# Transposes by DMA, side matmuls in halves, value batches in pairs: a fused transformer block on one core

## The chip, the core and the metric

The kernel runs on 1 core of one Trainium2 chip. The metric is the device time of one execution in microseconds: 1193.36 before the change, the median of 3 runs (1192.19 to 1194.55). The core has TensorE (PE, its weight loads are PEld), VectorE (DVE), ScalarE (ACT), GpSimd (POOL) and SyncE (SP, here the issuer of nearly all DMAs). Each engine works through its own stream of instructions in order; semaphores order them against each other.

## The reference, cut to what matters

The input x has 4096 rows of 256. Three residual steps follow each other (a macaron block):

```python
x = x + 0.5 * ffn(layernorm(x))
x = x + attention(layernorm(x))     # 16 heads of size 16, causal, 4096 x 4096 scores per head
x = x + 0.5 * ffn(layernorm(x))

# attention: k, q, v = x Wk', x Wq', x Wv'; k and q get a layernorm per head (gain, bias), times 256**-0.25
#            out = softmax(causal(q k')) v, then out Wo' + bo
# ffn:       base = x W' + b;  logits = x router', softmax, the two largest of 6, made to sum to 1
#            inner = x A' (7 experts of rank 16, one of them shared), weighed, times B', added to base
```

## The kernel before

**Chunks and stages.** The rows are cut into 8 chunks of 512 (4 tiles of 128). Around the attention of chunk c the kernel does side work for other chunks, in stages with names: `front` (first feed-forward: moments0, scale0, turn0, inner0, route0, weigh0, turnin0, outer0), `prepare` (moments1, scale1, turn1, qk, square and squares, roots, value, norm, heads), `output` (turnout, projout) and `back` (moments2 to outer1). While chunk c is in attention, the side work is `prepare(c+1)`, a front, `output(c-1)` and `back(c-2)`. The first two fronts and most of `prepare` of chunks 0 and 1 stand before any attention, in the prelude; the string PRELUDE gives its order.

**Attention.** The scores come in 1056 units; most are two heads times one tile of 128 keys times 512 queries. A unit is 2 score matmuls in f16 into two banks of PSUM, one exponential by ScalarE over 128 x 1024 (line 776) into a slot of `ring` (5 slots in f32), and later a share of a values batch: 4 heads, so two units, 8 recorded f32 matmuls (one values batch) that add into bank ACC. There are 544 batches. Scores stand two units ahead of the exponential, in 3 pairs of banks (SLOTS). The units of chunks 0 to 7 number 20, 52, 84, 116, 148, 180, 212 and 244.

**Order.** `schedule` writes one global order. For each unit: exp, mask, side stages of place 3u, scores(u+2), side stages of place 3u+1, values, side stages of place 3u+2. PLACES says for each chunk and each kind of side work at which place, in thirds of a unit, each stage stands. Every engine takes its part of each stage out of this one order, so a matmul of a side stage stands in PE's stream between scores and values.

**Transposing on PE.** `turn` (line 1232) transposes normed rows, f32, 128 x 256 pairs: four 128 x 128 transposes into one bank, twice per chunk and layer norm. `turn_inner` (line 1252) does four for the weighed inner product. The f32 result is then split into an f16 part and an f16 rest (`move_parts`, lines 846 and 848, the first by ScalarE in some chunks, line 765), because the side matmuls are done as three f16 products. `turn_heads` (line 1298) transposes q and k, VectorE gives them gain and bias (line 1013) and casts (1017), POOL makes the rest (537), SP writes the parts to DRAM and reads them back into `keys` and `queries`.

**Queues.** SP issues all these DMAs in the same global order and waits for the semaphore of each in that order. All side stages but those of the prelude and of the end share one PSUM bank (SIDE).

**The prelude.** VectorE does moments and `scale` (line 828); POOL squares qk (line 532) into the one buffer `sq`, and VectorE sums them (985), by turns. ScalarE squares the weights for their sizes (line 752), three at the start and four when stage sizes 1 comes. The first score follows the whole prelude.

## Time and profile before

| | before |
|---|---|
| median of 3 runs | 1193.36 us |
| span of the profiled execution | 1192.3 us |
| PE busy / PEld busy | 1104.1 / 359.6 us |
| ACT busy, of it exponentials | 1014.7, 982.2 us |
| DVE / POOL busy | 467.5 / 241.6 us |
| first exponential starts, last starts | 96.3, 1158.4 us |

The page gives for each engine the busy time and its share of the span, and the span in 40 slices with a digit each. A group's line has line, engine, operation, output<-input, shapes and count, then busy us and mean ns of one, then the idle time just before it and who ended that. The profiled execution has no time of its own beside its span; it is 1.1 us under the median.

### The profile page before, as it was taken

How to read it: one execution, taken by the hardware profiler on the slowest of the kernel's cores; microseconds unless marked ns; L12 is line 12 of the kernel's file. 1: busy time of each engine (PE TensorE's matmuls, PEld its weight loads, DVE VectorE, ACT ScalarE, POOL GpSimd, SP SyncE). 2: the span in 40 equal slices, each digit the busy share in tenths (PEclk: the TensorE clock that was granted, in tenths of full speed). 3: DMA queues.
4: the chain of work that ended last, by engine and by line, in shares of the span. 5: the costliest groups of instructions: out<-in, count | busy, mean ns of one | idle time of the engine just before them, and what ended most of it. 6: DMA issues, size and time to landing. Idle time of an engine off the chain costs nothing.

```text
span 1192.3 us, 22761 instructions
## 1 busy us (share of the span) xinstructions
PE 1104.1 (93%) x8884; PEld 359.6 (30%) x8884; DVE 467.5 (39%) x1181; ACT 1014.7 (85%) x1134; POOL 241.6 (20%) x377
## 2 busy tenths in 40 slices
PE   3758999999999999999999999999999999999994
PEld 3534333332323233232332232232222222222123
DVE  5678665554544353333333323423131222021114
ACT  3216788789888998999999999999999999999980
POOL 2236533222122211212022021012110101010100
PEclk9779999999999999999999999999999999999996
DMA  5022202003000300003000022000001100000000
GB/s 145 3 63 60 59 11 81 1 28 99 1 1 19 93 17 1 1 32 92 4 1 1 1 67 60 1 1 2 1 10 48 53 1 1 10 10 1 1 19 18
DMA packets 39608, 33.37 MB, mean 28 GB/s; under 512 B 8722, under 2 KB 39432, under 8 KB 39496
## 3 DMA queue, kind: packets, MB, share of 16 engines
q1 hardware_dynamic: 37364, 31.74, 9.0%
q8 instruction: 73, 1.20, 0.4%
q10 hardware_dynamic: 2132, 0.12, 0.1%
q14 instruction: 39, 0.32, 0.1%
HBM read 18.73 MB, written 12.85 MB: 26 GB/s over the span
## 4 chain that ended last, share of the span: by engine, by line
PE 72%; ACT 13%; issue 6%; DVE 6%; DMA 1%; POOL 1%; SPq 0%; ACTq 0%; DVEq 0%; POOLq 0%
PE ps L1190 68%; ACT ring L776 13%; PE ps L1232 2%; PE ps L1298 1%; DMA x<-in_x 1%; DVE st L807 1%; PE ps L1252 1%; DVE area L828 1%; DVE oT L1159 0%; POOL rstd L711 0%; POOL sq L532 0%; DVE x L980 0%; DVE ss L985 0%; DVE sq L1013 0%; ACT area L765 0%
## 5 line engine op out<-in xcount | busy, mean ns | idle before, releaser
L776 ACT ACTIVATE ring<-ps 128x1024 f32<-128x1024 f32 x1056 | 982.2, 1115 | 65.5 <-PE ps L1190 63.5
L1190 PE MATMUL ps<-ring,vf 128*17 128x512 f32 (+3 forms) x4608 | 559.4, 562 | 5.0 <-DVE oT L1159 4.4
L1190 PE MATMUL ps<-queries,keys 50*128 50x512 f16 (+3 forms) x2304 | 363.2, 366 | 22.1 <-ACT ring L776 4.9
L1190 PEld LDWEIGHTS ps<-queries,keys 50*128 50x128 f16 x2304 | 92.3, 93 | 475.3 <-ACT ring L776 437.3
L724 POOL TENSOR_SCALAR_AFFINE_SELECT ring<-ring 128x256 f32<-128x256 f32 (+1 forms) x224 | 103.9, 481 | 396.5 <-ACT ring L776 392.6
L1190 PEld LDWEIGHTS ps<-ring,vf 128*17 128x17 f32 x4608 | 79.7, 95 | 174.5 <-issue 144.2
L711 POOL TENSOR_TENSOR rstd<-var,minus_half 128x4 f32<-128x4 f32 x24 | 24.4, 1017 | 235.6 <-DVE var L813 235.4
L980 DVE SCALAR_TENSOR_TENSOR x<-ps,power,x 128x512 f32<-128x512 f32 x32 | 24.0, 750 | 110.7 <-PE ps L1190 110.7
L846 DVE CAST xnT<-ps 128x512 f16<-128x512 f32 x32 | 22.1, 691 | 100.0 <-PE ps L1232 100.0
L1190 PE MATMUL ps<-baseT,xnT 128*128 128x256 f16 x384 | 55.0, 283 | 3.9 <-DVE area L848 3.8
L1232 PE MATMUL ps<-ident,area 128*128 128x128 f32 x192 | 34.2, 311 | 20.0 <-DVE area L828 20.0
L765 ACT ACTIVATE xnT<-ps 128x512 f16<-128x512 f32 x16 | 9.6, 599 | 49.9 <-PE ps L1232 49.9
L1159 DVE STREAM_TRANSPOSE oT<-ps 128x512 f32<-128x512 f32 x32 | 22.9, 715 | 71.0 <-PE ps L1190 70.5
L1190 PE MATMUL ps<-qkT,xnT 128*128 128x512 f16 x192 | 48.7, 394 | 1.7 <-DVE xnT L848 1.5
L532 POOL TENSOR_TENSOR sq<-area 128x512 f32<-128x512 f32 x32 | 33.5, 1047 | 67.2 <-DVE ss L985 41.7
L1190 PEld LDWEIGHTS ps<-baseT,xnT 128*128 128x128 f16 x384 | 36.7, 101 | 19.2 <-issue 11.0
L828 DVE TENSOR_SCALAR area<-x,mv,rstd 128x256 f32<-128x256 f32 x96 | 36.9, 444 | 11.3 <-POOL rstd L711 11.3
L1013 DVE TENSOR_SCALAR sq<-ps,scaled 128x512 f32<-128x512 f32 x16 | 12.9, 806 | 70.1 <-PE ps L1298 70.1
L537 POOL TENSOR_TENSOR split<-sq,split 128x512 f16<-128x512 f32 x16 | 18.8, 1175 | 100.0 <-DVE split L1017 100.0
L807 DVE BATCH_NORM_STATS2 st<-x 128x6 f32<-128x256 f32 x96 | 33.5, 412 | 9.5 <-DMA x<-in_x 4.8
L1232 PEld LDWEIGHTS ps<-ident,area 128*128 128x128 f32 x192 | 23.6, 156 | 43.0 <-issue 36.9
L848 DVE TENSOR_TENSOR xnT<-ps,xnT 128x512 f16<-128x512 f32 x48 | 33.1, 691 | 7.6 <-ACT xnT L765 6.3
(153 smaller groups left out, 670.5 us busy)
## 6 DMA issues: line engine op xcount, KB each, us to landing
parts_d<-split SPq DMA_DIRECT2D x32, 256.0 KB, 2.6
keys<-parts_d SPq DMA_DIRECT2D x96, 64.0 KB, 2.3
queries<-parts_d SPq DMA_DIRECT2D x192, 32.0 KB
x<-in_x SPq DMA_DIRECT2D x8, 512.0 KB, 4.2
out_x<-x SPq DMA_DIRECT2D x16, 256.0 KB, 2.2
queries<-shift_d SPq DMA_DIRECT2D x64, 4.0 KB
ring<-in_base_W SPq DMA_DIRECT2D x1, 256.0 KB, 4.9
ring<-in_Wq SPq DMA_DIRECT2D x1, 256.0 KB, 3.8
```

Of the source, the lines that this page charges most:

```text
L532: e.tensor_tensor(sq[:, :], qn[:, n % TC, :], qn[:, n % TC, :], ALU.mult).then_inc(K.sq_ok, 1)
L711: pool.tensor_tensor(rstd[ln][:, :], var[ln][:, 0, :], minus_half[:, :].broadcast_to([P, TC]), ALU.pow).then_inc(main.rstd_ok[ln], 1)
L724: m = pool.affine_select(out=tiles[:, part, :], in_=tiles[:, part, :], compare_op=ALU.is_ge, fill=0.0, base=0, pattern=[[0, len(range(8)[p ...
L776: act.activation(probs[:, u % RING, :], bank(2 * (u % SLOTS), 2), ACTF.Exp, bias=0.0, scale=1.0).then_inc(exp_ok, 1)
L807: dve.bn_stats(st[ln][:, i, :], x[:, i, :]).then_inc(*own.up())
L828: m = dve.tensor_scalar(xn[ln][:, i, :], x[:, i, :], mv[ln][:, i, 0:1], rstd[ln][:, i:i + 1], ALU.subtract, ALU.mult)
L846: dve.tensor_copy(high, src).then_inc(*K.own.up())
L848: dve.tensor_tensor(low, src, high, ALU.subtract).then_inc(K.read, 1)
L980: dve.scalar_tensor_tensor(out=x, in0=bank(K.bank[key]).rearrange("p (n d) -> p n d", n=2), scalar=power[0][:, 5:6], in1=x, op0=ALU.mult, ...
L1159: dve.transpose(oT[:, :], bank(ACC)).then_inc(acc_read, 1)
L1190: return pe.matmul(o, lhsT, rhs, start=start, stop=stop, skip_group_check=True)
L1232: m = pe.transpose(b[:, ib * D + i * P:ib * D + (i + 1) * P], xn[ln][:, 2 * a + i, ib * P:(ib + 1) * P], ident[:, :])
```

## The change

- **Transposes by DMA.** `by_queue` says which: turn0 and turnin0 from chunk 3 on, turn1 from chunk 2 on, turn2 and turnin1 up to chunk 6. For these, DVE (ScalarE where it did before) makes the f16 part and rest from SBUF before the transpose, into the unused half of `area`, and SP issues one `dma_start_transpose` (`turn_rows`, `turn_hrows`) of 128 x 1024 f16. PE issues no transpose and waits for the landing before the next side matmul (`wait_turned`). POOL clears the unused columns first. `xnT` is laid out anew by tile.
- **Halves.** Side matmul stages (qk, value, projout, inner, outer) of later chunks are two stages each with places of their own.
- **Pairs.** `held_back` holds a values batch back until the next one, where HELD has a 1 (88 of them); `ring` gets a sixth slot, for which `split` falls from four buffers to two (a head block waits until the write of the block before the last has landed).
- **ScalarE in the prelude.** scale0 of chunks 0 to 2 and scale1 of chunk 0, the squares of chunk 0 from PSUM, the heads of chunk 0 (two passes each), and all seven weights' squares at the start. Squares use two buffers (`qT[n % 2]`).
- `addbo` stands behind the heads; PRELUDE and all of PLACES are new (the prelude's string has 100 entries and had 102; the half stages add positions).

```diff
-RING = 5
+SCALAR_SCALES, SCALAR_HEADS, SCALAR_SQUARES = (3, 1, 0), 1, 1
+QUEUED_FRONT, QUEUED_PREPARE, QUEUED_BACK = 3, 2, NC - 1
+RING = 6
...
+def by_queue(stage, n):
+    if stage in ("turn0", "turnin0"):
+        return (n[0] if stage == "turn0" else n) >= QUEUED_FRONT
+    if stage == "turn1":
+        return n[0] >= QUEUED_PREPARE
+    return stage in ("turn2", "turnin1") and (n[0] if stage == "turn2" else n) < QUEUED_BACK
+def halved(stage, n):
+    if stage == "qk":
+        return n >= 2 * TC
+    if stage == "value":
+        return n[0] >= 2
+    if stage == "projout":
+        return n[0] < NC - 1
+    if stage in ("outer0", "inner0"):
+        return (n[0] if stage == "outer0" else n) >= LONG
+    return stage in ("outer1", "inner1") and (n[0] if stage == "outer1" else n) < NC - 1
+def pieces(weight, stage, n):
+    if halved(stage, n):
+        yield weight / 2, stage + "half", n
+        weight /= 2
+    yield weight, stage, n
...
     for b in BLOCKS:
         yield 2.5, "heads", (c, b)
+    yield 0, "addbo", c
...
+def held_back(b):
+    c, g = BATCHES[b][:2]
+    i = b - (LAST_BATCH[NG * c + g] - TC * c - 2)
+    return i % 2 == 1 and HELD[c, g][i // 2] == "1"
...
-            values.append((u + (2 if BATCHES[b][3] else 1), b))
+            waiting.append(b)
+            if not held_back(b):
+                values.extend((u + (2 if BATCHES[b][3] else 1), q) for q in waiting)
+                waiting = []
...
+        (3, 0): "1000110",
+        (3, 1): "0000111",
+        (3, 2): "1101001",
+        (3, 3): "1111010",
...
-        split = sb("split", [P, 2, 4, CH], F16)
+        split = sb("split", [P, 2, 2, CH], F16)
...
-            if n >= TC and n % TC == 0:
-                e.wait_ge(K.high_ok, n)
-                e.wait_ge(K.low_ok, n)
+            squares_free(e, K, n)
             e.wait_ge(*K.done["qk", n])
-            e.tensor_tensor(sq[:, :], qn[:, n % TC, :], qn[:, n % TC, :], ALU.mult).then_inc(K.sq_ok, 1)
+            e.tensor_tensor(qT[n % 2][:, :], qn[:, n % TC, :], qn[:, n % TC, :], ALU.mult).then_inc(K.sq_ok, 1)
...
+            def turn_rows(K, ln, c, a):
+                sp.wait_ge(K.rows_ok[ln], 2 * turns_before(f"turn{ln}", c) + a + 1)
+                if c >= 1 and ln == 1:
+                    for n in range(TC * (c - 1), TC * c):
+                        sp.wait_ge(*K.done["qk", n])
+                    for i in range(2):
+                        sp.wait_ge(*K.done["value", (c - 1, i)])
+                elif c >= 1:
+                    sp.wait_ge(*K.done[f"outer{ln // 2}", (c - 1, 1)])
+                if ln == 2:
+                    sp.wait_ge(*K.done["projout", (min(c + 1, NC - 2), 1)])
+                sp.dma_start_transpose(xnT[ln][:, 2 * a:2 * a + 2, :, :, :].rearrange("p n s b t -> p (n s b) t"), parts_rows(ln, a)).then_inc(K.turned[ln][a], 16)
+            def turn_hrows(K, f, c):
+                sp.wait_ge(K.hrows_ok[f], turns_before(f"turnin{f}", c) + 1)
+                sp.dma_start_transpose(hT(K, f, c).rearrange("p n s t -> p (n s) t"), hrows(f)).then_inc(K.hturned[f], 16)
...
-            squares(range(3))
+            squares(range(NW))
             for stage, n in ORDER:
-                if (stage, n) == ("sizes", 1):
-                    squares(range(3, NW))
-                elif stage == "weight":
+                if stage == "weight":
                     dst, src = weight_target(n, 0)
                     act.wait_ge(main.w_turned, n + 1)
                     act.activation(dst, src, ACTF.Copy).then_inc(main.w_high, 1)
+                elif stage in ("scale0", "scale1") and n[0] < SCALAR_SCALES[int(stage[-1])]:
+                    ln, (c, a) = int(stage[-1]), n
+                    act.wait_ge(main.nm_ok[ln], c + 1)
+                    for i in range(2):
+                        t = 2 * a + i
+                        m = act.activation(normed(main, ln, c, a)[:, i, :], x_main(c)[:, t, :], ACTF.Identity,
+                                           bias=var[ln][:, 1, t:t + 1], scale=rstd[ln][:, t:t + 1])
+                    m.then_inc(main.xn_ok[ln], 1)
+                elif stage == "heads" and on_scalar(stage, n):
+                    c, b = n
+                    k, g = TC * c + BLOCKS.index(b), 2 * (b // 2)
+                    if k >= 2:
+                        act.wait_ge(main.low_ok, k - 1)
+                        act.wait_ge(main.parts_out[BLOCKS[(k - 2) % TC]], 16 * ((k - 2) // TC + 1))
+                    act.wait_ge(main.ss_ok, TC * (c + 1))
+                    act.wait_ge(main.bal_ok, 1)
+                    act.wait_ge(main.ready, main.use[stage, n])
+                    act.activation(split[:, 0, k % 2, :], bank(main.bank[stage, n]), ACTF.Identity, bias=scaled[:, g + 1:g + 2], scale=scaled[:, g:g + 1])
+                    act.activation(qT[k % 2][:, :], bank(main.bank[stage, n]), ACTF.Identity,
+                                   bias=scaled[:, g + 1:g + 2], scale=scaled[:, g:g + 1]).then_inc(main.read_act, 1)
                 elif stage in BANK_STAGES and on_scalar(stage, n):
-                    act.wait_ge(main.ready, main.use[stage, n])
-                    dst, src = moved(stage, n, main.bank[stage, n])
+                    if stage == "qk" and n < TC * SCALAR_SQUARES:
+                        squares_free(act, main, n)
+                        act.wait_ge(main.ready, main.use[stage, n])
+                        act.activation(qT[n % 2][:, :], bank(main.bank[stage, n]), ACTF.Square, bias=0.0, scale=1.0).then_inc(main.sq_ok, 1)
+                    if by_queue(stage, n):
+                        wait_rows(act, stage, n)
...
-                for i in (2 * a, 2 * a + 1):
-                    m = dve.tensor_scalar(xn[ln][:, i, :], x[:, i, :], mv[ln][:, i, 0:1], rstd[ln][:, i:i + 1], ALU.subtract, ALU.mult)
+                if K is main and c < SCALAR_SCALES[ln]:
+                    if a == 0:
+                        dve.scalar_tensor_tensor(out=var[ln][:, 1, :], in0=mv[ln][:, :, 0], scalar=-1.0, in1=rstd[ln][:, :],
+                                                 op0=ALU.mult, op1=ALU.mult).then_inc(K.nm_ok[ln], 1)
+                    return
+                if a == 1 and ln != 1 and K.queue(f"turn{ln}", (c, a)):
+                    dve.wait_ge(K.rows_ok[ln], 2 * turns_before(f"turn{ln}", c) + 1)
+                for i in range(2):
+                    n = 2 * a + i
+                    m = dve.tensor_scalar(normed(K, ln, c, a)[:, i, :], x[:, n, :], mv[ln][:, n, 0:1], rstd[ln][:, n:n + 1], ALU.subtract, ALU.mult)
                 m.then_inc(K.xn_ok[ln], 1)
...
-                high, src = moved(stage, n, K.bank[stage, n])
-                low = moved(stage, n, K.bank[stage, n], 1)[0]
+                high, src = moved(K, stage, n)
+                low = moved(K, stage, n, 1)[0]
+                queued, i = K.queue(stage, n), int(stage[-1])
                 if K.scalar(stage, n):
                     dve.wait_ge(*K.high[stage, n])
                 else:
-                    dve.wait_ge(K.ready, K.use[stage, n])
+                    if queued:
+                        wait_rows(dve, stage, n)
+                    else:
+                        dve.wait_ge(K.ready, K.use[stage, n])
                     dve.tensor_copy(high, src).then_inc(*K.own.up())
                     dve.wait_ge(*K.own.at())
-                dve.tensor_tensor(low, src, high, ALU.subtract).then_inc(K.read, 1)
+                done = K.read if not queued else K.rows_ok[i] if stage in ("turn0", "turn1", "turn2") else K.hrows_ok[i]
+                dve.tensor_tensor(low, src, high, ALU.subtract).then_inc(done, 1)
...
                 key = (f"turn{ln}", (c, a))
+                if K.queue(*key):
+                    return
...
+            def wait_turned(K, ln, c):
+                for a in range(2):
+                    if K.queue(f"turn{ln}", (c, a)):
+                        pe.wait_ge(K.turned[ln][a], 16 * turns_before(f"turn{ln}", c + 1))
+                    else:
+                        pe.wait_ge(*K.done[f"turn{ln}", (c, a)])
...
+            def project(K, n, parts=(0, 1)):
+                c = n // TC
+                b = side_bank(K, ("qk", n), 0 in parts)
+                if 0 in parts:
+                    pe.wait_ge(K.w_ok, 5)
+                    wait_turned(K, 1, c)
+                for ib in parts:
+                    m = mm_parts(b, lambda s: xnT[1][:, n % TC, s, ib, :], lambda s: qkT[:, s, ib, :], ib == 0, ib == 1)
                 if 1 in parts:
                     m.then_inc(K.ready, 1)
```

## Rows read from the trace of the kernel before

**Rows 1.** The page: busy time, and the group of the exponentials.

```profile
PE 1104.1 (93%) x8884; PEld 359.6 (30%) x8884; DVE 467.5 (39%) x1181; ACT 1014.7 (85%) x1134; POOL 241.6 (20%) x377
...
L776 ACT ACTIVATE ring<-ps 128x1024 f32<-128x1024 f32 x1056 | 982.2, 1115 | 65.5 <-PE ps L1190 63.5
```

**Rows 2.** Windows, by stage; columns in the first line.

```profile
core 0: us, PE busy (x) PEld busy (x) DVE busy (x) ACT busy (x) POOL busy (x), PEclk, DMA share, GB/s
0.00:95.40 95.40, 53.27 (x320) 40.72 (x320) 65.65 (x211) 23.39 (x48) 30.28 (x48) 0.80 0.26 70
95.40:200.00 104.60, 97.08 (x898) 39.23 (x902) 70.77 (x168) 82.60 (x97) 52.12 (x84) 0.98 0.18 53
200.00:600.00 400.00, 394.26 (x3279) 124.54 (x3272) 180.55 (x439) 362.04 (x394) 87.99 (x134) 1.00 0.10 30
...
600.00:1160.60 560.60, 544.68 (x4297) 143.74 (x4295) 135.53 (x325) 544.69 (x594) 69.11 (x109) 1.00 0.05 15
...
1160.60:1192.30 31.70, 14.79 (x96) 11.35 (x96) 15.01 (x41) 2.02 (x4) 2.10 (x3) 0.71 0.05 17
```

**Rows 3.** Waits of all engines, the one of the exponentials.

```profile
ACT ring L776 <- PE ps L1190: 63.5, 88, 3.3
```

**Rows 4.** Timeline of PE, 480 to 500 us: start, length, what.

```profile
489.14 1.05 PE L1190 MATMUL ps<-ring,vf 128*17 128x512 f32 x8
490.13 1.47 PE L1190 MATMUL ps<-qkT,xnT 128*128 128x512 f16 x6
491.53 0.61 PE L1190 MATMUL ps<-queries,keys 50*128 50x512 f16 x4
492.07 1.05 PE L1190 MATMUL ps<-ring,vf 128*17 128x512 f32 x8
...
499.71 0.62 PE L1190 MATMUL ps<-ring,vf 128*17 128x512 f32 x4
```

**Rows 5.** Timeline of ACT, 480 to 500 us, idle time in brackets.

```profile
492.02 5.61 ACT L776 ACTIVATE ring<-ps 128x1024 f32<-128x1024 f32 x6 [0.80 <-PE ps L1190]
```

**Rows 6.** Groups of PE, 95.4 to 200 us.

```profile
L1232 PE MATMUL ps<-ident,area 128*128 128x128 f32 x16 | 2.6, 285 | 0.2 <-DVE area L828 0.2
L1252 PE MATMUL ps<-ident,area 128*113 128x128 f32 x8 | 1.8, 368 | 0.0
```

**Rows 7.** The same, 200 to 600 us.

```profile
L1232 PE MATMUL ps<-ident,area 128*128 128x128 f32 x72 | 11.8, 286 | 0.2 <-DVE area L828 0.2
L1252 PE MATMUL ps<-ident,area 128*113 128x128 f32 x24 | 4.2, 295 | 0.0
```

**Rows 8.** The same, 600 to 1160.6 us.

```profile
L1232 PE MATMUL ps<-ident,area 128*128 128x128 f32 x56 | 9.2, 287 | 0.0
...
L1252 PE MATMUL ps<-ident,area 128*113 128x128 f32 x20 | 3.5, 296 | 0.0
```

**Rows 9.** Timeline of the prelude, PE and DVE.

```profile
25.72 0.56 PE L1190 MATMUL ps<-sums,xnT 128*128 128x4 f32 x2 [4.05 <-ACT sq L752]
...
42.52 4.71 DVE L828 TENSOR_SCALAR area<-x,mv,rstd 128x256 f32<-128x256 f32 x8 [0.71 <-POOL rstd L711]
...
77.14 0.80 DVE L1013 TENSOR_SCALAR qT<-ps,scaled 128x512 f32<-128x512 f32 x1
```

**Rows 10.** DMA issues: KB each, median us from issue to landing.

```profile
parts_d<-split SPq DMA_DIRECT2D x32, 256.0 KB, 2.6
...
shift_d<-att SPq DMA_DIRECT2D x2, 128.0 KB, 7.7
```

**Rows 11.** Groups of DVE, whole run: f16 part from SBUF, rest from SBUF.

```profile
L1176 DVE CAST xnT<-area 128x512 f16<-128x512 f32 x14 | 7.0, 497 | 0.5
...
L1178 DVE TENSOR_TENSOR xnT<-area,xnT 128x512 f16<-128x512 f32 x14 | 10.0, 715 | 0.5
```

**Rows 12.** Timeline of DVE and POOL at the start, route to weighed product.

```profile
21.31 0.24 DVE L908 SCALAR_TENSOR_TENSOR lg<-ps,power,rb 128x24 f32<-128x24 f32 x1 [0.60 <-PE ps L1190]
...
25.51 0.94 POOL L522 TENSOR_TENSOR area<-area,wt 128x448 f32<-128x448 f32 x1
```

More of the change, by code:

```diff
@@ L89, in front @@
     yield 1.7, f"moments{ln}", (c, 1)
-    for a in range(2):
-        yield 0.8, f"scale{ln}", (c, a)
-    for a in range(2):
-        yield 1.5, f"turn{ln}", (c, a)
-    yield 2, f"inner{f}", c
+    if by_queue(f"turn{ln}", (c, 0)):
+        for a in range(2):
+            yield 0.8, f"scale{ln}", (c, a)
+            yield 1.5, f"turn{ln}", (c, a)
+    else:
+        for a in range(2):
+            yield 0.8, f"scale{ln}", (c, a)
+        for a in range(2):
+            yield 1.5, f"turn{ln}", (c, a)
+    yield from pieces(2, f"inner{f}", c)
     for k in range(3):
@@ L99, in front @@
     for a in range(2):
-        yield 2.5, f"outer{f}", (c, a)
+        yield from pieces(2.5, f"outer{f}", (c, a))
 def prepare(c):
@@ L115, in prepare @@
     for n in tiles:
-        yield 1.8, "qk", n
+        yield from pieces(1.8, "qk", n)
         if n > tiles[0]:
@@ L119, in prepare @@
         yield 0.3, "square", n
-    yield 1.8, "value", (c, 0)
+    yield from pieces(1.8, "value", (c, 0))
     yield 0.7, "squares", tiles[-1]
@@ L123, in prepare @@
         yield 1.3, "roots", (c, k)
-    yield 1.8, "value", (c, 1)
+    yield from pieces(1.8, "value", (c, 1))
     for n in tiles:
@@ L135, in output @@
     for stage, a in (("turnout", 1), ("projout", 0), ("projout", 1)):
-        yield 1.5, stage, (c, a)
+        yield from pieces(1.5, stage, (c, a))
 def back(c):
@@ L316, in on_scalar, with high_heads @@
         return n == NC - 1
+    if stage == "heads":
+        return n[0] < SCALAR_HEADS
     return stage == "qk" and n // TC <= 2
+def high_heads(k):
+    return max(0, k - TC * SCALAR_HEADS)
 class Step:
@@ L569, in moved, with wait_rows, turns_before @@
             return vf[:, n0:n0 + 2, :, 0:HS], bank(b).rearrange("p (n h c) -> p n h c", n=2, c=HS)
+        def wait_rows(e, stage, n):
+            if stage in ("turnin0", "turnin1"):
+                e.wait_ge(main.hw_ok[int(stage[-1])], weighed(main, int(stage[-1]), n))
+            else:
+                c, a = n
+                e.wait_ge(main.xn_ok[int(stage[-1])], 2 * c + a + 1)
+                if a == 1 and stage != "turn1":
+                    e.wait_ge(main.turned[int(stage[-1])][0], 16 * turns_before(stage, c + 1))
+        def turns_before(stage, c):
+            return sum(by_queue(stage, m if stage in ("turnin0", "turnin1") else (m, 0)) for m in range(c))
         @block.sync
@@ L1000, in norm @@
                 dve.wait_ge(K.sq_ok, n + 1)
+                if K is main and n < TC * SCALAR_SQUARES:
+                    dve.wait_ge(*K.done["qk", n])
                 dve.wait_ge(*K.own.at())
@@ L1190, in mm, with side_bank @@
                 return pe.matmul(o, lhsT, rhs, start=start, stop=stop, skip_group_check=True)
-            def side_bank(K, key):
-                if K.last[key]:
+            def side_bank(K, key, first=True):
+                if K.last[key] and first:
                     pe.wait_ge(*K.last[key])
@@ L1283, in value @@
-            def value(K, c, a):
-                b = side_bank(K, ("value", (c, a)))
-                pe.wait_ge(K.w_ok, 6)
-                for i in range(2):
-                    pe.wait_ge(*K.done["turn1", (c, i)])
-                for i in range(2):
+            def value(K, c, a, parts=(0, 1)):
+                b = side_bank(K, ("value", (c, a)), 0 in parts)
+                if 0 in parts:
+                    pe.wait_ge(K.w_ok, 6)
+                    wait_turned(K, 1, c)
+                for i in parts:
@@ L1299, in turn_heads, with rest @@
                 m.then_inc(K.ready, 1)
+            def rest(K, stage, n):
+                return (1,) if K is main and halved(stage, n) else (0, 1)
             def front_and_heads(K, stage, n):
@@ L1391, in values @@
                 m.then_inc(pv, 1)
-            before = [q for q in ORDER[:ORDER.index(("scores", 0))] if q[0] in BANK_STAGES]
+            before = [q for q in ORDER[:ORDER.index(("scores", 0))] if q in main.bank]
             side_last = [main.done[[q for q in before if main.bank[q] == b][-1]] for b in START_BANKS[1:]]
```

315 lines of the change are left out of this document (207 added, 108 removed).

## The prediction

> **What bounds the kernel now.** I read the page first, then windows by stage, the waits, and short stretches of the timeline. PE is busy for 93% of the span and ACT for 85% [rows 1], so PE looks like the bound. The windows divide that. From the first exponential at about 95.4 us to 200 us ACT is idle for 104.6 - 82.6 = 22.0 us, from 200 to 600 us for 400 - 362.0 = 38.0 us, and from 600 to 1160.6 us for only 560.6 - 544.7 = 15.9 us [rows 2]. In the late part the exponentials themselves are the limit; in the early part the side work crowds PE. The wait of the exponentials for PE's scores is 63.5 us in 88 pieces [rows 3], nearly all of those 75.9 us. Ahead of them lie 95.4 us of prelude, and 31.7 us of a serial end behind.
>
> What a bubble looks like: a values batch takes 1.05 us with the next matmul 0.99 us after its start, the scores of two units 0.54 us (491.53 to 492.07), a qk stage 1.40 us (490.13 to 491.53) [rows 4]. Together 2.93 us, while ACT uses up two units in 2 x 5.61 / 6 = 1.87 us; without side work PE needs 1.53 us. So each such stage puts PE 1.06 us behind, and each free batch wins 0.34 us back. ACT had 0.80 us of idle just there [rows 5].
>
> The floor that follows: 982.2 us of exponentials [rows 1] are not touched. The most there is to win after the start is 75.9 us.
>
> **Part by part.**
>
> *Transposes off PE.* Turns go from 36 of 48 places and inner turns from 12 of 16. All recorded ones of line 1232 after 95.4 us go: 2.6 us up to 200 us [rows 6], 11.8 us up to 600 us [rows 7], 9.2 us after [rows 8]. Of line 1252 half of the first 1.8 us stays (chunk 2), then 4.2 and 3.5 us go. Relief of PE: 3.5, 16.0 and 12.7 us.
>
> *Pairs.* Four recorded f32 matmuls take 0.62 us and eight 1.05 us, so four more cost 0.43 us; eight with the next start at 0.99 hold 0.13 us that is paid once per batch, on going from f16 to f32 [rows 4]. Going back costs between nothing and as much. I take 0.22 us for both, times 88 held batches = 19.4 us on PE: 9 of them in chunks 0 and 1 (2.0 us), some 40 from 200 to 600 us (chunk 2 has 4, chunks 3 and 4 have 15 and 17, the rest is the beginning of chunk 5; 8.8 us), 39 later (8.6 us). The price: two batches hold PE for 2 x 0.99 - 0.13 = 1.85 us, while ACT has two units or 1.87 us ahead. That fits only just, and where a side half stands beside it, a short bubble comes. The sixth slot of the ring keeps the held probabilities; alone it is worth nothing.
>
> *Halves.* They take nothing off PE. They replace 2.93 by two batches of 2.23 us, each only 0.36 us over the 1.87, which one free batch repays (0.34). I count 3 us for them up to 600 us, within 0 and 10.
>
> *What is left of the idle time.* 200 to 600 us: relief 16.0 + 8.8 = 24.8, of which I count 22 as time (some falls where ACT is not waiting), with halves 3: 25 of 38.0 us. Up to 200 us: relief 3.5 + 2.0, and DVE's work of the prelude no longer runs on; 6 of 22.0 us (bounds 2 and 12). After 600 us: relief 12.7 + 8.6 = 21.3 is more than ACT's whole idle time of 15.9; I count 10 (bounds 4 and 14), because bubbles of pairs stay.
>
> *Prelude.* The squares of the last four weights no longer stand in sizes 1, for which PE waited 4.05 us; they move to the start, where ACT is idle. 16 scales leave DVE (12 of scale0, 4 of scale1); a run of eight took 4.71 us, so at most 16 x 0.59 = 9.4 us, less because ACT now does them one behind the other with its own passes between. Four heads of 0.80 us and a cast each leave DVE too, at least 3.2 us [rows 9]. DVE is busy for 65.7 of 95.4 us, ACT for 23.4 [rows 2]. Against it: the third and fourth head block now wait until the first and second have landed, 2.6 us [rows 10], with ACT's turn copies of chunk 1 queued behind them. The prelude's matmuls run at a granted clock of 0.80 in the mean, so partly at 1.2 GHz [rows 2], and fewer waits might raise that; I leave it out. I take 8 us, between -3 and 14.
>
> *The DMA that replaces the transpose.* The trace of before has no transposing DMA. A plain one of the same 256 KB lands after 2.6 us in the median; the slowest to land here, 128 KB to DRAM in bad pieces, takes 7.7 us [rows 10]. 48 are issued, by SP, in order; queued behind each are head writes, fetches, stores of x. PE has 30 waits for them (18 pairs of turns, 12 inner turns), with the next scores queued behind. The new places give the cover. From the first half of the side product after which DVE may begin to the matmul that needs the landing lie at least 12.3 units of 0.935 us by PLACES, 11.5 us (outer0 to qk for chunk 5; inner0 to outer0 for chunk 6 are 12.7). The chain in it, for an inner turn: route and weighing 5.1 us (21.31 to 26.45) [rows 12], part and rest 0.50 + 0.72 us [rows 11], landing 2.6 us: 8.9 us; I put the other kinds at the same. So it is hidden up to a landing of some 5.2 us. At 7.7 us it would come 2.5 us late at the 6 tightest places, of which ACT has 1.87 us ahead: 6 x 0.6 = 4 us. I take 0. DVE's own cost falls a little (0.50 instead of 0.69 us for a part from PSUM) and is covered; it is under half busy after 200 us.
>
> The Trainium skill (Advanced Engine Details and Errata, X-Bar Transpose (TRN2)) says that transposing DMAs are as fast as regular ones on trn2, while DMA: Bandwidth & Descriptors (Latency and other measured facts) gives 261 GB/s for one with a non-contiguous middle dimension. By the first the landing is that of a plain DMA; by the second the bytes alone take an estimated 1.0 us. By either the sum stays as it is; no row here shows a transposing DMA.
>
> *End, and addbo.* The last chunk keeps PE's transposes: 31.7 us stay. addbo only moves behind the heads on POOL; its reader comes a chunk later. 0.
>
> **Sum.** 8 + 6 + 25 + 10 = 49 us. The profiled execution is 1192.3 us, the median 1193.4; 1193.4 - 49 = 1144.4 us.
>
> **Rivals.**
>
> *B: the bubbles are not the load.* PE's busy share is stretched by its own waits (scores wait for ACT's slots), so less load buys less time; the new places and the pairs' bursts keep the bubbles. For it: from 600 us on PE is busy for 97% though a free batch needs 1.53 of 1.87 us. Against: the bubble stands exactly behind a side stage [rows 5]. Half of 41 us, (6 + 25 + 10), and 3 of the prelude: 1193.4 - 20.5 - 3 = 1170 us. The Trainium skill (Perfetto Trace Analysis, Identifying the Most-Contended Engine) says that matmul busy share is a poor measure and ACT's a fair one; the trace agrees for the late part (ACT 97%). By that rule PE's load is not what bounds, and this is the outcome.
>
> *C: nearly all bubbles close.* The late idle falls to 3 us, the middle to 8, the early to 12, and the prelude gives 10: 13 + 30 + 10 + 10 = 63, so 1130 us. For it: relief exceeds the late idle time.
>
> *D: the transposed rows land late (slower).* Place: PE's 30 waits. If a landing takes L us more than the cover, PE stands L at each and ACT loses L - 1.9. To eat 49 us it must lose 1.6 us at each, L = 3.5; with the cover of the tightest places (5.2 us) that is a landing of 8.7 us, waits in SP's and DVE's queues included, and more where the places are wider. At 2 us beyond that: 30 x 3.6 = 108, less 49: 1252 us; just beyond, 1200 us. I take 1215 us. Against: only plain landings of worse pieces reach 7.7 us.
>
> *E: nothing happens,* C's gains and D's losses in balance or the turning done as before: 1193 us.
>
> **How the numbers follow.** Forecast (1133 to 1160 us) 0.59, B (1160 to 1185) 0.17, C (1115 to 1133) 0.15, D 0.07, E 0.02. A change within 0.2% (2.4 us) can't be told from none. Faster: 0.59 + 0.17 + 0.15 = 0.91, of which 0.01 goes to the border of B with no change: 0.90. Same 0.02 + 0.01 = 0.03, slower 0.07. The range reaches from 1122, well into C, to 1174, half-way through B; 0.05 lies under it and 0.14 over it.
>
> **What would show it.** No matmul of line 1232's kind between 110 and 1160 us but for chunk 2's; 48 transposing DMAs, landing in under 5 us; PE waits for them of under 5 us in all; 88 runs of 16 recorded 512-column f32 matmuls, each 0.2 us shorter than two batches; ACT idle from 200 to 600 us about 13 us and after it about 6; first exponential at about 88 us; 31.7 us behind the last one as before. The prediction is wrong if the first exponential is not earlier, if waits for landings reach 1.9 us many times, or if ACT idles as much at pairs as it did at side stages.

## The result, and the profile after

The changed kernel takes 1173.43 us (median of 4 runs, 1172.14 to 1173.78), the kernel before 1193.95 us in the same comparison: a ratio of 0.9819, 95% interval 0.9807 to 0.9831. It is faster by 20.5 us where I forecast 49. (The ratio of the two medians is 0.9828, inside the interval. Between two of the versions below, differences of 1 to 2 us are inside their intervals.) The size is that of rival B; its reason has to be shown.

The page of the changed kernel, busy times and exponentials, against [rows 1]:

```profile
PE 1068.1 (91%) x8692; PEld 339.7 (29%) x8692; DVE 453.4 (39%) x1161; ACT 1034.1 (88%) x1162; POOL 238.6 (20%) x385
...
L981 ACT ACTIVATE ring<-ps 128x1024 f32<-128x1024 f32 x1056 | 986.8, 1084 | 45.9 <-PE ps L1413 42.7
```

PE has 36 us less busy time and the span is 20 us shorter. The windows, cut where the first and the last exponential of this kernel lie (92.87 and 1139.0 us), against [rows 2], columns as there:

```profile
0.00:92.90 92.90, 51.64 (x326) 39.42 (x328) 55.87 (x193) 38.57 (x77) 24.28 (x43) 0.82 0.28 76
92.90:200.00 107.10, 98.56 (x910) 39.34 (x906) 75.06 (x175) 87.78 (x100) 52.59 (x85) 0.97 0.24 63
...
1139.00:1172.00 33.00, 15.94 (x104) 11.53 (x104) 15.01 (x41) 2.03 (x5) 2.09 (x3) 0.73 0.05 16
...
200.00:600.00 400.00, 386.82 (x3269) 119.42 (x3272) 182.07 (x453) 371.41 (x401) 92.57 (x146) 1.00 0.19 46
600.00:1139.00 539.00, 515.11 (x4094) 129.97 (x4086) 125.37 (x302) 534.29 (x583) 67.10 (x108) 1.00 0.10 24
```

ACT's idle time is 19.3 us up to 200 us (22.0 before), 28.6 us from 200 to 600 us (38.0) and 4.7 us after (15.9). PE is idle for 13.2 us from 200 to 600 us, where it was idle for 5.7. So in the middle, where I expected 25 us, ACT won 9, and PE got 7.5 us more of idle time.

The waits of the changed kernel (who waited for whom, us in total, times, longest), against [rows 3]:

```profile
ACT ring L981 <- PE ps L1413: 42.7, 83, 3.3
...
PE ps L1413 <- ACT ring L981: 23.9, 46, 1.3
...
PE ps L1413 <- DMA xnT<-area: 2.9, 3, 1.6
...
PE ps L1413 <- DMA area<-area: 0.2, 1, 0.2
```

The transposing DMAs land in time: PE waits 3.1 us for them in all (DVE 10.8 us, beside other work). Their issues (count, median us to landing), against [rows 10]:

```profile
xnT<-area SPq DMA_TRANSPOSE x36, 3.1
area<-area SPq DMA_TRANSPOSE x12, 3.1
```

What new bubbles look like: PE's timeline, where two halves of the outer product stand directly behind each other, twice, because chunk 4's front must end before its preparation (start, length, what), and ACT's at the same time:

```profile
317.60 0.82 PE L1413 MATMUL ps<-baseT,xnT 128*128 128x256 f16 x6 [0.24 <-DMA area<-area]
...
319.24 0.49 PE L1413 MATMUL ps<-bT,area 113*128 113x256 f16 x3
319.66 0.39 PE L1413 MATMUL ps<-queries,keys 50*128 50x512 f16 x2
320.58 0.83 PE L1413 MATMUL ps<-baseT,xnT 128*128 128x256 f16 x6 [0.52 <-DVE x L1198]
...
322.65 0.39 PE L1413 MATMUL ps<-queries,keys 50*128 50x512 f16 x2
```

```profile
320.15 1.02 ACT L981 ACTIVATE ring<-ps 128x1024 f32<-128x1024 f32 x1 [1.48 <-PE ps L1413]
323.14 1.02 ACT L981 ACTIVATE ring<-ps 128x1024 f32<-128x1024 f32 x1 [1.97 <-PE ps L1413]
```

Two blocks of 2 us, with one unit of scores between them: 3.45 us of idle ACT. PE's lead, the two units of scores that stand ready for ACT, lasts only 1.87 us.

**Which blocks ACT waits behind.** For each piece of ACT's idle time before an exponential that PE ended (0.15 us or more), I take the longest run of side matmuls that ended in the 3 us before that exponential. In the kernel before, 56.8 of 62.7 us stand behind the 90 side blocks of over 1.2 us, and only 2.3 us, in 4 pieces, behind the 75 blocks of under 0.8 us, PE's transposes among them. In the changed kernel 30 blocks of over 1.2 us are left, with 19.0 of 42.0 us; 22.2 us stand behind the 149 shorter ones. In the run `neither` (below), without halves and pairs, 59.2 of 63.9 us stand behind 90 long blocks again.

**Chunk by chunk.** From the starts of the 1056 exponentials in each trace (unit number as in the kernel's order) come the durations of the attention of each chunk. From the start of each recorded matmul to the next one comes what of a chunk PE spent on scores, values and side stages; waiting inside a kind counts with it. In us:

```
                        first   chunk 0    1     2      3      4      5      6      7
before                   96.3      31.3  62.9  91.5  121.9  148.1  175.0  202.5  229.8
changed                  92.9      30.2  65.1  87.3  120.0  147.1  171.2  198.1  227.1
light_turns              95.9      29.9  62.1  90.6  121.6  148.8  176.4  202.5  229.8
neither                  94.2      27.6  67.7  88.1  120.7  148.0  175.6  204.3  231.3
dma_old                  96.6      29.1  88.0  90.5  127.9  147.5  176.2  202.2  229.5

chunk 6: scores / values / side     before  68.3 / 104.8 / 29.4     changed  67.9 / 104.2 / 25.8
                                light_turns 70.4 / 104.8 / 27.3     neither  74.6 / 104.8 / 24.6
                                dma_old     72.7 / 104.8 / 24.6
```

The 20 us: 3.4 in the prelude, 1.1 in chunk 0, -2.2 in chunk 1, then 4.2, 1.9, 1.0, 3.8, 4.4 and 2.7; the end is as before.

The first two of these come from one profiled execution each, and they scatter. The changed kernel and the runs no_halves, qk_whole, spread and pe_turns below have the same instructions up to the start of chunk 1, yet their first exponentials start at 92.9, 95.5, 92.9, 93.7 and 92.9 us, and chunk 0 takes 30.2, 27.6, 28.0, 28.1 and 27.6 us. Differences of up to 2.7 us between two kernels in these two columns say nothing by themselves. The eight kernels with the new prelude whole start at 92.9 to 95.5 us, 93.7 in the mean; the kernel before, light_turns and more_scores, which share the old one, at 96.3, 95.9 and 96.7. So the new prelude is earlier, by some 2.6 us.

### The profile page after: what moved, and what is told of

Read it like the earlier page. It is cut to its first block, busy times and chain, and to the rows that moved or that the text cites. A ratio compares the mean times of both kernels' runs of the same rounds, so it can differ in the third digit from the quotient of the medians.

```text
span 1172.0 us, 22468 instructions
## 1 busy us (share of the span) xinstructions
PE 1068.1 (91%) x8692; PEld 339.7 (29%) x8692; DVE 453.4 (39%) x1161; ACT 1034.1 (88%) x1162; POOL 238.6 (20%) x385
## 2 busy tenths in 40 slices
DMA packets 90294, 45.93 MB, mean 39 GB/s; under 512 B 59410, under 2 KB 90120, under 8 KB 90184
## 3 DMA queue, kind: packets, MB, share of 16 engines
q1 hardware_dynamic: 88052, 44.33, 14.9%
## 4 chain that ended last, share of the span: by engine, by line
PE 70%; ACT 13%; DVE 7%; issue 5%; DMA 2%; POOL 1%; SPq 1%; ACTq 0%; POOLq 0%; DVEq 0%
PE ps L1413 68%; ACT ring L981 12%; PE ps L1539 1%; DMA xnT<-area 1%; DVE st L1012 1%; PE ps L1465 1%; ACT area L945 0%; DVE oT L1381 0%; DVE area L1066 0%; DMA ring<-in_Wo 0%; DVE xnT L1066 0%; DVE x L1198 0%; DVE area L1222 0%; DMA x<-in_x 0%; POOL rstd L890 0%
## 5 line engine op out<-in xcount | busy, mean ns | idle before, releaser
L981 ACT ACTIVATE ring<-ps 128x1024 f32<-128x1024 f32 x1056 | 986.8, 1084 | 45.9 <-PE ps L1413 42.7
L1413 PE MATMUL ps<-ring,vf 128*17 128x512 f32 (+3 forms) x4608 | 544.0, 563 | 4.6 <-POOL ring L904 3.2
L1413 PEld LDWEIGHTS ps<-ring,vf 128*17 128x17 f32 x4608 | 88.8, 96 | 196.0 <-issue 152.4
L1198 DVE SCALAR_TENSOR_TENSOR x<-ps,power,x 128x512 f32<-128x512 f32 x32 | 24.0, 751 | 181.5 <-PE ps L1413 181.4
L1049 DVE COPY area<-ps 128x512 f32<-128x512 f32 x20 | 13.8, 691 | 94.4 <-PE ps L1413 94.4
L1066 DVE TENSOR_TENSOR area<-area 128x512 f16<-128x512 f32 (+1 forms) x48 | 36.4, 759 | 4.2 <-ACT area L970 2.7
L1041 DVE TENSOR_SCALAR area<-x,mv,rstd 128x256 f32<-128x256 f32 x80 | 30.7, 432 | 15.7 <-POOL rstd L890 15.0
L1413 PE MATMUL ps<-bT,area 113*128 113x256 f16 x192 | 32.2, 280 | 1.5 <-DVE area L1066 1.5
L656 POOL TENSOR_TENSOR sq<-area 128x512 f32<-128x512 f32 x14 | 14.6, 1039 | 91.4 <-DVE area L1049 87.8
L1407 DVE SCALAR_TENSOR_TENSOR x<-ps,power,x 128x512 f32<-128x512 f32 x16 | 12.0, 749 | 52.4 <-PE ps L1413 52.4
L671 POOL TENSOR_TENSOR split<-qT,split 128x512 f16<-128x512 f32 x16 | 18.6, 1160 | 59.2 <-DVE split L1239 58.3
L1539 PE MATMUL ps<-ident,area 128*128 128x128 f32 x128 | 22.4, 303 | 8.7 <-DVE area L1222 8.7
```

What stands on the lines that cost most here:

```text
L656: e.tensor_tensor(qT[n % 2][:, :], qn[:, n % TC, :], qn[:, n % TC, :], ALU.mult).then_inc(K.sq_ok, 1)
L671: e.tensor_tensor(split[:, 1, k % 2, :], qT[k % 2][:, :], split[:, 0, k % 2, :], ALU.subtract).then_inc(K.low_ok, 1)
L981: act.activation(probs[:, u % RING, :], bank(2 * (u % SLOTS), 2), ACTF.Exp, bias=0.0, scale=1.0).then_inc(exp_ok, 1)
L1041: m = dve.tensor_scalar(normed(K, ln, c, a)[:, i, :], x[:, n, :], mv[ln][:, n, 0:1], rstd[ln][:, n:n + 1], ALU.subtract, ALU.mult)
L1066: dve.tensor_tensor(low, src, high, ALU.subtract).then_inc(done, 1)
L1198: dve.scalar_tensor_tensor(out=x, in0=bank(K.bank[key]).rearrange("p (n d) -> p n d", n=2), scalar=power[0][:, 5:6], in1=x, op0=ALU.mult, ...
```

## The experiments

Ratios are to the kernel before, run on the same chip; 1% is 12 us. The changed kernel is at 0.9819.

**light_turns.** The kernel before, its transposes made cheap:

```diff
                 pe.wait_ge(K.xn_ok[ln], 2 * c + a + 1)
+                if K is main and {0: c >= 3, 1: c >= 2, 2: c < NC - 1}[ln]:
+                    mm(b, identh[:, :], qkT[:, 0, 0, :], True, True).then_inc(K.ready, 1)
+                    return
```

(and the same in `turn_inner`.)

> The kernel before, where each group of four f32 transposes that the change gives to the DMA (36 of the turns, 12 of the inner turns) is one f16 matmul of 512 columns on weight data instead; what the side products compute from there is no longer the block's result. It takes some 0.37 us off PE at each of 48 places, 18 us in all, in the old positions. Load theory (PE's total work crowds the exponentials): 10 to 16 us faster than before, about 1180 us. Granularity theory (a bubble of ScalarE comes only behind a side block longer than PE's lead, 1.4 us for qk and 2.1 us for outer; a transpose group of 0.6 us never makes one): 0 to 4 us faster, 1189 to 1193 us.

Ratio 0.9996 (0.9987 to 1.0006), 1195.11 us. The whole wait of ACT for PE is the same as in [rows 3], 63.5:

```profile
ACT ring L776 <- PE ps L1190: 63.8, 88, 3.3
```

Chunk 6 takes 202.5 us as before. Side stages cost PE 2.1 us less there, and scores take 2.1 us more, which fits PE waiting that much longer for a free slot. Some 18 us of work taken off in pieces of 0.37 us, from blocks of 0.6 us, are worth nothing here. It is not the whole relief of the change (48 groups of 0.59 us from start to start, 28 us); dma_old below takes that off.

**no_pairs.** The changed kernel without held batches:

```diff
-    return i % 2 == 1 and HELD[c, g][i // 2] == "1"
+    return False
```

> The changed kernel with no values batch held back (HELD read as all 0). Load theory: 88 pairs took 0.22 us each off PE, so 10 to 15 us slower than the changed kernel's 1173 us. Granularity theory: 0 to 3 us slower, because most of the 88 pairs stand where ScalarE does not wait. A third possibility: the pairs' bursts of 1.85 us make bubbles of their own, then it is 1 to 4 us faster.

0.9890 (0.9873 to 0.9906), 1182.59 us: 8.5 us slower than the changed kernel. More than the granularity theory said.

**no_halves.** Each halved stage whole, at the place of its second half:

```diff
-                side.setdefault(3 * UNIT0[c] + place, []).append((stage, n))
+                if not stage.endswith("half"):
+                    side.setdefault(3 * UNIT0[c] + place, []).append((stage, n))
...
-                return (1,) if K is main and halved(stage, n) else (0, 1)
+                return (0, 1)
```

> The changed kernel with each halved side stage done whole at the place of its second half. Granularity theory: the bubbles behind qk and outer come back, 8 to 15 us slower than 1173 us. Load theory: PE's work is the same, within 2 us of 1173.

0.9973 (0.9962 to 0.9984), 1192.03 us: 18 us slower than the changed kernel, with the same work.

**neither.** Both edits.

> The changed kernel without halves and without pairs: the new positions, the DMA transposes and ScalarE's share are left. If halves (18 us) and pairs (9 us) add up: 1173 + 27, about 1201 us, slower than before. If they cover the same bubbles: 1190 to 1195 us.

0.9973 (0.9961 to 0.9984), 1191.84 us. So of the changed kernel's 1.8%, the new positions, all DMA transposes and ScalarE's share make 0.3% together (3 us), and the earlier start of the new prelude is most of that. Pairs alone (no_halves against this) add nothing; halves alone (no_pairs) 0.8%; both 1.5%. They don't add up singly: each is worth more beside the other. All these runs take a part out of an order that was made with all parts in it, so they give a part's worth in this order only. In chunk 6 side stages cost PE 4.8 us less than before, and scores took 6.3 us more.

**pe_turns.** As no_halves, and `by_queue` returns False.

> As the kernel without halves, and all transposes back on PE and none by DMA. Against the kernel without halves, load theory: 28 us more on PE, 15 to 22 us slower. Granularity theory: 2 to 6 us slower.

1.0548 (1.0530 to 1.0565), 1260.19 us: 69 us slower than no_halves. Neither theory had that. The waits:

```profile
ACT ring L984 <- PE ps L1416: 116.6, 137, 6.2
...
PE ps L1468 <- DVE area L1044: 20.4, 6, 7.3
...
PE ps L1468 <- DVE xnT L1069: 11.2, 10, 1.5
```

Back in PE's queue, the transposes (line 1468) wait for DVE's normed rows (area) and for DVE to empty the one side bank (xnT), and the scores behind them wait too. Of the 20.4 us for normed rows 12.2 us lie in the prelude; behind the first exponential it is 8.2 us in 4 pieces. There ACT waits 116.6 us for PE, against 57.6 in no_halves, twice for over 6 us. In this order transposing on PE costs 69 us more than by DMA. How much of that is PE's own work (some 28 us) and how much the waits, this run does not divide.

**dma_old.** The reverse: the changed kernel's DMA transposes in the old order:

```diff
-SCALAR_SCALES, SCALAR_HEADS, SCALAR_SQUARES = (3, 1, 0), 1, 1
+SCALAR_SCALES, SCALAR_HEADS, SCALAR_SQUARES = (0, 0, 0), 0, 0
...
-    if halved(stage, n):
+    if False:
...
-    return i % 2 == 1 and HELD[c, g][i // 2] == "1"
+    return False
...
-                return (1,) if K is main and halved(stage, n) else (0, 1)
+                return (0, 1)
```

PRELUDE and PLACES are those of the kernel before, and addbo is yielded behind turn1 as there. The changed kernel's ring, split buffers and squares stay.

> The changed kernel's DMA transposes (with its six ring slots, two split buffers and double-buffered squares) in the order and the positions of the kernel before: no halves, no pairs, ScalarE's new share of the prelude undone but for the weights' squares. Theory 'bubbles come only behind long blocks': the DMA takes 28 us off PE and buys nothing there, 0 to 4 us faster than before, as light_turns (0.9996) did. Load theory: 15 us or more faster. Theory 'the landings are late': slower, by up to 30 x the lateness over PE's lead.

1.0240 (1.0213 to 1.0266), 1222.91 us, slower. Chunks 1 and 3 take 25.1 and 6.0 us more, chunks 2 and 4 to 7 the same as before within 1.2 us. PE's waits for DMA in chunk 1 (126 to 214 us), and what SP issued ahead of the one that ends last:

```profile
PE ps L1409 <- DMA area<-area: 10.4, 1, 10.4
PE ps L1409 <- DMA xnT<-area: 10.2, 2, 7.1
```

```profile
195.23 1.30 SPq L769 DMA_DIRECT2D queries<-parts_d  x3
...
198.57 1.24 SPq L769 DMA_DIRECT2D queries<-parts_d  x3
199.84 0.28 SPq L770 DMA_DIRECT2D queries<-shift_d  x1
```

The 10.4 us: DVE finished the rows at 192.59 us, the transpose is issued at 201.78 us and lands at 204.84, and PE goes on at 204.98. It lands in 3 us, but it stood for 9.2 us behind head writes and fetches in SP's queue. The other 10.2 us are mostly not that: PE stands from 134.57 us, DVE finishes the two halves of the rows at 134.82 and 136.73, and they are issued at 136.85 and 138.46 and land at 140.13 and 141.57; for the last piece the rows are ready at 158.37, issued at 158.40, landed at 161.48. There the rows are late, and the 3.1 us of the landing stand uncovered. So rival D is a real mechanism in this order: once through the queue, twice through late rows and the landing.

The run also shows the whole relief. In chunk 6 PE's side stages take 4.8 us less than before, its scores 4.4 us more, and the chunk is as long as before (202.2 for 202.5 us).

**dma_late.** As dma_old, with QUEUED_FRONT and QUEUED_PREPARE 5.

> As dma_old (old positions, no halves, no pairs), but the fronts and preparations of chunks 3 and 4 (and prepare of chunk 2) are transposed on PE again; the DMA does those from chunk 5 on and the back stages. In dma_old the attention of chunk 1 took 88.0 us for 62.9 before and that of chunk 3 127.9 for 121.9, all others the same as before. Theory 'the landing is late only where the old positions leave no cover': both losses go, the same time as before within 0.3%. Rival 'DMA turns cost everywhere': a part of the 2.4% stays.

1.0043 (1.0026 to 1.0060), 1200.58 us. Chunk 1 is back at 63.5 and chunk 3 at 123.0, but chunk 4, now the first with DMA turns for the next chunk, takes 153.1 for 148.1 us. Most of the loss went, one such place remains; my 0.3% was missed by little.

**halves_old, halves_wide.** Halves in the old order, on top of dma_old one unit apart, on top of dma_late four units apart (a helper inserts the first half, moves the rest of that chain back, and leaves a stage whole where another chain's bank use lies between):

```diff
+                    end = place + 3
...
+                        items.insert(i, [stage + "half", n, place])
+                        for q in items[i + 1:]:
+                            q[2] = max(q[2], end)
```

In halves_wide the 3 is 12.

> As dma_old, and 84 of the 86 side stages that the change halves are halved here too: the first half stays at the old place, the second comes one unit (3 thirds) later. Granularity theory: halves are worth as much as they are in the changed kernel (its own loss without them was 18 us), so 10 to 20 us faster than dma_old. Theory 'the new positions are what counts': within 5 us of dma_old.

1.0459 (1.0432 to 1.0485), 1249.14 us, 26 us slower than dma_old.

> As dma_late, with 69 of 86 stages halved, the second half 4 units (12 thirds) behind the first instead of 1 unit. Theory 'a half pays if free batches lie between it and the next, in which PE wins back its lead of 0.34 us per batch': 8 to 18 us faster than dma_late. Rival 'halves pay only with all positions chosen together, since what follows in the chain is pushed back': same as dma_late or slower, as halves_old was (2% slower than dma_old).

1.0396 (1.0379 to 1.0413), 1243.39 us, 43 us slower than dma_late; chunks 2 to 4 lose 10, 18 and 12 us against it. Only in chunk 6 is it faster, 201.3 for 202.2 us. What the chain needs later comes later, and that costs more than the halves bring. In an order that was not made for them halves failed twice; that they help needs the new order, and only there was it shown.

**spread.** The changed kernel, PE's side stages from chunk 2 on kept 5 thirds of a unit apart, moved back by at most 9.

> The changed kernel with the side stages of PE from chunk 2 on kept at least 5 thirds of a unit apart, each moved back by at most 9 thirds. If bubbles of bunched halves (some 3 us at 318 to 323 us in chunk 3) are most of what is left and the chains have the room: 2 to 8 us faster than the changed kernel. If the moved stages come too late for what follows: slower.

0.9893 (0.9876 to 0.9909), 1182.45 us: 9 us slower. Chunk 4 gains 1.1 us, chunk 3 loses 6.7 us and chunk 2 3.5. The bunches are deadlines.

**all_pairs.** `held_back` returns `i % 2 == 1`.

> The changed kernel with every second batch held back wherever the code allows, 256 instead of 88. If a pair is worth its 0.22 us of PE everywhere: faster than the changed kernel by 5 us or more. If a pair only pays where the positions of the side work were chosen for it and costs a bubble elsewhere (two batches hold PE for 1.85 us, all of its lead): slower by 5 us or more.

1.0065 (1.0039 to 1.0091), 1202.61 us: 29 us slower than the changed kernel. ACT waits for PE 57.8 us in 115 pieces, for 42.7 in 83. A pair has its price, as the 1.85 us against 1.87 said.

**scalar_off, heads_back.** ScalarE's share undone ((0, 0, 0), 0, 0), and its heads alone ((3, 1, 0), 0, 1).

> The changed kernel with the scales, squares and heads of the first block back on VectorE and POOL (the weights' squares stay at the start). Prelude theory: ScalarE's share bought 3 to 4 us of the 20, so about 1177 us with the first exponential at 95 to 98 us. Rival: the prelude gained by the weights' squares and the second squares buffer alone, then within 1 us of the changed kernel.

0.9841 (0.9816 to 0.9865), 1175.91 us, 2.5 us slower. The interval overlaps that of the changed kernel, and against the kernel before in the same comparison it is 20.0 us faster, where the changed kernel is 20.5: no difference is shown. The first exponential comes at 97.2 us, later than in any of the eight kernels with the new prelude; its chunk 0 takes 27.6 us, which lies within the scatter told above.

> The changed kernel with the heads of the first block back on VectorE; scales and squares stay on ScalarE. With all three back it was 2.5 us slower, but its chunk 0 took 27.6 us instead of 30.2, the time in which ScalarE's head passes wait for a landing. If the heads are what costs there: 1 to 2.5 us faster than the changed kernel, the best version. If VectorE then delays the second block: 0 to 3 us slower.

0.9808 (0.9793 to 0.9823), 1171.18 us. It can't be told from the changed kernel (0.9807 to 0.9831). Its chunk 0 takes 30.1 us, but the 27.6 us that this run was to explain are scatter. No version was shown to beat the changed kernel.

**more_scores.** The kernel before with the first score matmul of every fourth unit done twice:

```diff
-                for h, j, q0, w, b, col in blocks:
+                for h, j, q0, w, b, col in (blocks[:1] if u % 4 == 0 else []) + blocks:
```

> The kernel before with the first score matmul of every fourth unit done twice (the second overwrites the first, the result is the same): 264 more f16 matmuls of some 0.22 us, 58 us more work for a PE that the page shows busy for 93%. Load theory (PE's work is what takes the time): 35 us or more slower. Theory 'PE's busy time holds its own waiting, only blocks longer than its lead cost': 0.22 us per two batches fits into the 0.34 us that each free batch leaves, 0 to 15 us slower, the loss near the side blocks.

1.0187 (1.0169 to 1.0205), 1216.62 us: 22 us for 58 us of estimated work, between the two. Of PE and ACT from 200 to 600 us:

```profile
200.00:600.00 400.00, 397.33 (x3294) 127.25 (x3298) 178.45 (x434) 354.42 (x385) 87.50 (x133) 1.00 0.10 31
```

PE was busy for 394.3 us there before, and could still take the work of 264 matmuls in the whole run at 38% of its estimated length. So load is not without effect. Of ACT's waits for PE, 73.0 of 80.1 us stand behind the 90 long side blocks, where it was 56.8: the added work is paid there. Behind blocks of under 0.8 us it is 3.3 us, for 2.3. Work taken away from those short blocks (light_turns) is worth nothing.

**qk_whole.** Only qk and value whole.

> The changed kernel with only qk and value whole again (36 of the 86 halves undone, at the second's place); outer, inner and projout stay halved. Without any halves it lost 18 us. If every block counts by its length over PE's lead: qk 1.40 us is over it by 1.06 against two halves, outer 2.07 us by 1.7, so qk and value take a third, 5 to 8 us slower than 1173. If the longest blocks alone count: 0 to 3 us.

0.9865 (0.9842 to 0.9888), 1176.45 us by its median, 3 us slower, by the ratio 5.5 us. Both expected ranges touch this. With outer, inner and projout halved the larger part of the halves' 18 us stays; their blocks are the longest (outer 2.07 us).

## Why the prediction was wrong

By its own steps:

- *Transposes off PE, and "relief 24.8, of which I count 22 as time": this is the step that failed.* The relief is there (PE's side work in chunk 6 fell from 29.4 to 25.8 us). Its worth as load is about nothing: light_turns gives 0.9996 in the old order; dma_old, with the whole relief, has chunks 4 to 7 as long as before within 1.2 us; neither, with everything but halves and pairs, gives 0.9973. A transpose group holds PE for 0.6 us, and a batch leaves 0.34 us; that fits into the two units of lead. I had that sum for qk on the page and didn't make it for the transposes. ACT's idle time says the same: 2.3 of 62.7 us behind all short blocks. Even as load the relief was too high: I added busy times, 32.2 us in all, where the starts give 28.
- *PE busy 98% is no load.* The busy time of scores holds the wait for ACT's slot, since PE can't run more than two units ahead. What PE is freed of it gives back as waiting. Rival B said this and gave 1170 us. The Trainium skill (Perfetto Trace Analysis, Identifying the Most-Contended Engine) calls matmul busy share a poor measure of how close a kernel is to its roofline, because pipelined instructions look smaller. light_turns agrees that it is a poor measure, for another reason: here the share holds PE's own waiting. But B's "less load buys half" is too kind for the transposes and wrong for the halves.
- *Halves: 3 us, within 0 and 10.* They are the largest term: 10 us alone, 18 beside the pairs, in this order. The sum per stage was near (with a half of qk it is 0.75 + 0.99 + 0.54 = 2.28 us, for 2.23), and the size was wrong. ACT waits 56.8 us behind 90 long blocks before, 0.63 us each; the halves leave 30 of them. My reading, which no run tests: I priced a half as if one free batch always had to repay it; with the lead full at the start, the first 0.3 us of a block costs nothing, and halving uses that twice.
- *Pairs: counted as 19.4 us of PE.* Worth 8.5 us with the halves, nothing without them, and harmful where not chosen (all_pairs). In the trace a pair takes 1.91 us for 2 x 1.05, as worked out: sixteen in a row, from PE's timeline of the changed kernel:

```profile
296.09 1.91 PE L1413 MATMUL ps<-ring,vf 128*17 128x512 f32 x16
```

- *Prelude: 8 us.* 3.4 us. DVE's busy time fell by 9.8 us, but ACT's took its place in the chain: eight scales take it 4.04 us in a row (4.71 on DVE). The wait of PE in sizes 1 [rows 9] went, and others were late next: PE waits 9.0 us in two pieces for ACT's scales, and 4.88 us at 24.94 us for POOL's weighed product. ACT's third head block comes 3.67 us after ACT's last work; the first head write was issued at 66.42 us and the block starts at 70.57, and the write lands at 70.49, which fits the wait for the landing that I had named. It landed after 4.1 us, not the 2.6 us that I took. heads_back, with these blocks on DVE, is no slower and no faster, so that wait costs nothing that can be seen. The 3.4 us, or 2.6 by the means above, are inside the range given (-3 to 14), the value was too high.

The two waits of PE in the changed kernel (who waited for whom), and its row at 24.94 us:

```profile
PE ps L1465 <- ACT area L945: 9.0, 2, 5.2
```

```profile
24.94 1.17 PE L1488 MATMUL ps<-ident,area 128*113 128x128 f32 x4 [4.88 <-POOL area L646]
```

- *Up to 200 us: 6 us.* About -1: chunk 0 gained 1.1, chunk 1 lost 2.2 (65.1 for 62.9; 66.8 in no_pairs, 66.5 in scalar_off). The first of these is within the scatter. The second is not: chunk 1 takes 65.1 us or more in every version of the new order and 62.1 to 64.1 in the old one with PE's transposes. Neither the pairs nor ScalarE's share nor the halves (65.7 in no_halves) lengthened it; which of the rest did is left open.
- *After 600 us: 10 us.* ACT's idle time fell by 11.2 us. Right in size, but that is luck: by light_turns, dma_old and neither (whose chunks 5 to 7 are not shorter than before) it is the halves and pairs, not the relief, that did it.
- *The landing is hidden.* Right: 3.1 us in the median, 3.1 us of waits in all. That this holds by the new positions only, dma_old showed.
- *The floor.* An exponential behind a busy engine takes 0.904 us (median of start to start), one after a pause 1.02. So the 982.2 us are not fixed; without any pause they would be 1056 x 0.904 = 954.6, an estimate. Each bubble costs its idle time and 0.12 us more. The changed kernel's exponentials are busy for 986.8 us, no less than before: a pause too short to show as idle counts as busy, so the idle times understate what is lost.
- *The end.* From the last exponential's end to the end of the span: 32.9 us before (1159.4 to 1192.3), 33.0 after (1139.0 to 1172.0).

A smaller misreading of mine: 63.5 of 75.9 us are five sixths, not "nearly all".

Not settled: why halves and pairs are worth more together (18 us) than singly (10 and 0), what either is worth in an order made for it alone, and the loss in chunk 1. A look at subsets of HELD by chunk would be the next step.

## What to carry to other kernels

An engine that feeds the bound one through a few buffers can show as almost fully busy and still not be bound by its load: what it is freed of comes back as waiting. Ask of each piece of its side work not only how much it is in sum but how long it blocks, against the lead that the buffers give. Here cutting the long blocks in two was worth more than removing work that fits. Length is not all: work added beside long blocks is paid (more_scores), and in the changed order 22.2 of 42.0 us of idle time stand behind short blocks, for which no run shows the reason. An order planned for one set of operations is not the order for another: the same DMA transposes saved 69 us against PE's in the new order and cost 29 us in the old one, where they waited in SP's queue or landed uncovered. And a difference of 2 us in the prelude needs more than one profiled execution of each kernel.

## What the runs showed of the hardware

- A transposing DMA of 128 x 1024 f16, SBUF to SBUF, lands 3.1 us after its issue in the median, where a plain one of 256 KB takes 2.6. The Trainium skill (Advanced Engine Details and Errata, X-Bar Transpose (TRN2)) calls them as fast as regular ones; the trace agrees but for 0.5 us. The plain one goes to DRAM; no run has one of this size from SBUF to SBUF. All packets rise from 39,608 to 90,294, most under 512 B, and the share of the 16 engines from 9.0 to 14.9%, without a delay for the others: head writes still land in 2.6 us in the median.
- A group of matmuls takes some 0.1 us beyond its matmuls when another kind follows. To the next start, eight f32 ones of the values take 0.99 us and sixteen 1.84 (medians of 326 and 79 groups). The change from f16 to f32 is not needed for it, as I had it in the prediction: three f16 ones of the outer product take 0.33 us before more f16 ones of the same product and 0.43 before f16 scores (medians of 12 and 42), and two scores take 0.32 us whether f32 values or f16 side products follow.
